# Mixed stage reordered, with the transposition of the first maxima as a fill of the PSUM ring

## The reference

```python
x = x + conv_attn(group_norm(x))          # L0: 6 heads of 16, 1024 tokens, biases rel_h and rel_w on the scores
t = tokens(x)
t = t + causal_attn(layer_norm(t))        # L1: 6 heads of 16, keys after the query masked out
t = t + moe(layer_norm(t))

def moe(x):                               # 4 experts, 96 -> 384 -> 96
    probs  = softmax(x @ gate_w + gate_b)
    masked = probs * top2_mask(probs)
    masked = masked / (sum(masked) + 1e-9)
    h = gelu(x @ w1[e] + b1[e])           # for every expert e and every token
    y = h @ w2[e] + b2[e]
    return sum_e masked[..., e] * y[e]
```

## Time and profile before

| | us |
|---|---|
| runs of the kernel before, median of 3 | 2209.66 |
| lowest and highest of them | 2201.82, 2210.24 |
| the profiled execution | 2204.84 |
| its span, first to last instruction | 2203.0 |
| TensorE busy, of that span | 1855.9 (84%) |
| VectorE busy | 1255.3 (57%) |
| ScalarE busy | 1121.6 (51%) |
| mean granted TensorE clock | 0.933 of full |

### The profile page before, as it was taken

How to read it: one execution, slowest core, us unless ns; L and a number is a source line. 1 busy time by engine, 2 the same in 40 slices (tenths; PEclk the granted TensorE clock), 3 DMA queues, 4 the chain that set the end, 5 groups by cost and what they waited for, 6 DMA issues and landing times.

```text
span 2203.0 us, 28891 instructions
## 1 busy us (share of the span) xinstructions
PE 1855.9 (84%) x9314; PEld 743.8 (34%) x9408; DVE 1255.3 (57%) x2512; ACT 1121.6 (51%) x1423; POOL 141.7 (6%) x68
## 2 busy tenths in 40 slices
PE   0279568998899988998889988999889988999848
PEld 0123223343333432343333433344323433334324
DVE  5384367736665566736675466645676456744611
ACT  0326434675456734566446734567346744555423
POOL 0000000200020000200011000200002000200020
PEclk9669769999999999999999999999899999999979
DMA  1702530263004430163002530063202530002100
GB/s 44 134 10 53 91 72 21 50 97 65 21 18 92 57 77 11 47 110 65 22 18 56 89 80 11 18 115 64 42 22 49 96 65 13 18 10 54 28 10 7
DMA packets 55741, 111.43 MB, mean 51 GB/s; under 512 B 17687, under 2 KB 18904, under 8 KB 54041
## 3 DMA queue, kind: packets, MB, share of 16 engines
q1 hardware_dynamic: 54040, 109.06, 26.3%
q10 hardware_dynamic: 1536, 0.30, 0.1%
HBM read 61.82 MB, written 34.60 MB: 44 GB/s over the span
## 4 chain that ended last, share of the span: by engine, by line
PE 67%; DVE 18%; issue 4%; ACT 4%; DMA 4%; SPq 1%; POOL 0%; DVEq 0%; POOLq 0%; ACTq 0%
PE psOM L629 15%; PE psS L574 12%; PE psT L607 8%; PE psT L606 7%; PE psT L741 6%; DVE mx L1236 6%; PE psS L755 4%; PE psT L609 3%; PE psT L536 3%; DVE mrow L1338 2%; DVE x L1347 2%; DVE qb L1365 1%; DMA qr<-negb 1%; PE psOM L561 1%; PE psT L545 1%
## 5 line engine op out<-in xcount | busy, mean ns | idle before, releaser
L968 ACT ACTIVATE probs<-psT 128x1024 f32<-128x1024 f32 (+7 forms) x768 | 622.6, 837 | 535.2 <-PE psT L607 265.9
L1236 DVE TENSOR_REDUCE mx<-psS 128x1 f32<-128x512 f32 (+3 forms) x1152 | 704.2, 643 | 305.2 <-PE psS L574 225.1
L607 PE MATMUL psT<-qb,kb 97*128 97x512 f32 x768 | 416.1, 586 | 6.9 <-DMA qb<-negr 5.9
L629 PE MATMUL psOM<-probs,v 128*32 128x512 f32 (+3 forms) x2688 | 386.2, 560 | 22.6 <-ACT probs L968 12.0
L574 PE MATMUL psS<-ka,qa 128*128 128x512 bf16 x722 | 283.4, 401 | 22.1 <-DVE mx L1236 14.0
L606 PE MATMUL psT<-qa,ka 128*128 128x512 bf16 x720 | 278.2, 386 | 11.4 <-DVE resid L1225 4.0
L741 PE MATMUL psT<-xf,w1s 97*128 97x512 f32 x384 | 193.8, 633 | 4.2 <-ACT probs L1025 2.4
L1365 DVE TENSOR_TENSOR qb<-psOM,qa 32x768 fp32r<-32x768 f32 x128 | 121.8, 952 | 127.7 <-ACT qa L1008 126.0
L609 PE MATMUL psT<-qr,kr 97*128 97x512 bf16 (+3 forms) x576 | 185.6, 349 | 5.3 <-DMA qr<-negb 1.6
L755 PE MATMUL psS<-probs,w2s 128*96 128x512 f32 x384 | 187.9, 612 | 0.0
L574 PEld LDWEIGHTS psS<-ka,qa 128*128 128x128 bf16 x768 | 71.6, 98 | 301.3 <-DVE mx L1236 265.1
(11 more groups left out here) (143 smaller groups left out, 1598.8 us busy)
## 6 DMA issues: line engine op xcount, KB each, us to landing
scr<-split SPq DMA_DIRECT2D x32, 576.0 KB, 4.3
scr<-qb SPq DMA_DIRECT2D x16, 768.0 KB, 6.7
qr<-scr SPq DMA_DIRECT2D x48, 192.0 KB, 6.8
au<-ot SPq DMA_DIRECT2D x192, 32.0 KB, 2.0
lb<-ot SPq DMA_DIRECT2D x192, 32.0 KB, 2.0
qr<-scr SPq DMA_DIRECT2D x48, 128.0 KB, 4.3
kr<-scr SPq DMA_DIRECT2D x48, 128.0 KB, 7.3
qa<-scr SPq DMA_DIRECT2D x32, 128.0 KB, 3.8
```

The costliest lines, as they stand in the source:

```text
L607: last = mm(o[:, a:b], kb[:, h, ks], qb[:, h, a:b], start=False, stop=True)
L629: last = mm(psO[j:j + 2 * HD, a - c * HALF:HALF], v[:, kt, 2 * p + hh, :], probs[:, (2 * kt + hh) % 4, a:(c + 1) * HALF], start=kt == 0, s ...
L968: A(probs[:, n % 4, q0:T], psT[:, t_slot(ts, m), q0:T], ACT.Exp).then_inc(t_free, 1)
L1236: V.reduce_max(mx[layer][:, p % 2, (h % 2) * NT + t, kc:kc + 1], psS[:, s_bank(st, fill), 0:max_cols(layer, t, kc)], AX).then_inc(s_free, 1)
```

## The change

`MIX` gets a new order, and a new step `tmax`: the transposition of the maxima of pair 0, until now the first instruction of the attention into `psM`, becomes a fill of psT in the mixed stage, and ScalarE negates the row from there and sends it. Behind it come u11, d11 and b3, so the last expert's group stands behind the last maxima. LEAD becomes 0: the eight maxima that ran in front of the scores are made within the first pair, 24 in it in place of 16. The wait for `y_free` moves from the start of the attention to the first value product, `values(0, 0)`. The other hunks are the counts of the semaphores that follow from it.

```diff
@@ -49,7 +49,7 @@
 
 
 STAGES = ("p_gn", "p_qkv0", "gn", "attn1", "p_rel", "lead", "turn", "attn0", "qkv0", "attn0b", "norm", "mix")
-LEAD = 8
+LEAD = 0
 QKV_AT = 2 * NT + 2
 
 
@@ -77,9 +77,9 @@
             for w in text.split()]
 
 
...
+MIX = seq("gate gates u0 u1 R0 d0 H0 L0 H1 L1 v0 u2 d1 v1 ln den R1 u3 d2 u4 H2 L2 u5 res H3 d3 nrm L3 u6 d4 d5 tr R2 H4 L4 q0 q1 lev V0 d6 V1 "
+          "u7 H5 L5 R3 u8 d7 H6 L6 H7 L7 u9 b0 d8 u10 b1 m0 m1 m2 m3 d9 m4 m5 m6 m7 d10 m8 m9 m10 b2 m11 m12 m13 m14 m15 tmax u11 "
+          "d11 b3")
 
 
 def there(stage, kind):
@@ -213,7 +213,7 @@
 
 def att_m(layer, p):
 
-    return ("attn1", p) if layer else ("attn0", p - 1) if p else ("lead", 0)
+    return ("attn1", p - 1) if layer else ("attn0", p - 1) if p else ("lead", 0)
 
 
 def next_layer0(it):
@@ -579,10 +579,7 @@
 
             def transpose_max(it, layer, p):
                 ms, n = att_m(layer, p)
-                if layer == 1 and p == 0:
-                    pe.wait_ge(t_free, upto("t_free", it, ms, 0))
-                else:
-                    pe.wait_ge(rowmax, upto("rowmax", it, ms, p if layer else n + 1))
+                pe.wait_ge(rowmax, upto("rowmax", it, ms, n + 1))
                 pe.wait_ge(m_free, upto("m_free", it, ms, n))
                 mm(psM[0:2 * NT, 0:P], mrow[:, p % 2, :], ident, is_transpose=True, start=True,
                    stop=True).then_inc(m_full, 1)
@@ -617,6 +614,8 @@
 
                     q0 = q_from(layer, kt)
                     if kt == 0:
+                        if layer == 1 and p == 0:
+                            pe.wait_ge(y_free, upto("y_free", it, st, 0))
                         pe.wait_ge(o_free, upto("o_free", it, st, p))
                     for hh in range(2):
                         ts, n = att_t(layer, (p * NT + kt) * 2 + hh)
@@ -633,8 +632,6 @@
                 n = PER_PAIR[layer]
                 lead = layer == 1 and next_lead(it)
                 if layer == 1:
-                    pe.wait_ge(y_free, upto("y_free", it, st, 0))
-                    transpose_max(it, 1, 0)
                     pe.wait_ge(l1_in, upto("l1_in", it, "attn1", 0))
                     for fill in range(LEAD):
                         max_scores(it, st, fill)
@@ -661,7 +658,7 @@
                     if layer == 0:
                         pe.wait_ge(negmax_in, upto("negmax_in", it, st, 16 * p))
                     else:
-                        pe.wait_ge(negmax_in, upto("negmax_in", it, st, 16 * (p + 1)))
+                        pe.wait_ge(negmax_in, upto("negmax_in", it, st, 16 * p))
                     for kt in range(NT):
                         for hh in range(2):
                             scores(p, kt, hh, between)
@@ -824,6 +821,16 @@
                         if n == 0:
                             pe.wait_ge(l1_first, upto("l1_first", it, "mix", 192))
                         first_maxima(it, "mix", n)
+                    elif what == "tmax":
+                        first_rows(it, "mix")
+
+            def first_rows(it, st):
+
+                fs = fills(st, kind_of(it))
+                reduced = len([f for f in fs[:fs.index(("max", 2 * NT - 1)) + 1] if not by_act(f)])
+                pe.wait_ge(t_free, upto("t_free", it, st, reduced))
+                o = take_mixed(it, st, ("tmax", 0))
+                mm(o[0:2 * NT, 0:P], mrow[:, 0, :], ident, is_transpose=True, start=True, stop=True).then_inc(t_full, 1)
 
             def group_means(it, st):
                 pe.wait_ge(gstat, upto("gstat", it, st, 1))
@@ -935,13 +942,24 @@
             def neg_max(it, layer, p):
                 ms, n = att_m(layer, p)
                 act.wait_ge(m_full, upto("m_full", it, ms, n + 1))
-                act.wait_ge(negmax_in, upto("negmax_in", it, ms, 16 * max(p - 1, 0) if layer else 0))
+                act.wait_ge(negmax_in, upto("negmax_in", it, ms, 16 * max(p - 2, 0) if layer else 0))
                 A(negm[layer][:, p % 2, :], psM[0:2 * NT, 0:P], ACT.Copy, scale=-1.0).then_inc(m_free, 1)
                 act.wait_ge(m_free, upto("m_free", it, ms, n + 1))
                 row = (qb_raw, qr)[layer][C:C + 1, 2 * p:2 * p + 2, :]
                 act.dma_start(row.rearrange("o h (t q) -> o (h t) q", q=P),
                               negm_raw[layer][:, p % 2, :]).then_inc(negmax_in, 16)
 
+            def first_negated(it, st):
+
+                fs = fills(st, kind_of(it))
+                fill = fs.index(("tmax", 0))
+                act.wait_ge(t_full, upto("t_full", it, st, fill + 1))
+                act.wait_ge(negmax_in, upto("negmax_in", it, st, 0))
+                A(negm[1][:, 0, :], psT[0:2 * NT, t_slot(st, fill), 0:P], ACT.Copy, scale=-1.0).then_inc(ta_free, 1)
+                act.wait_ge(ta_free, upto("ta_free", it, st, len([f for f in fs[:fill + 1] if by_act(f)])))
+                act.dma_start(qr[C:C + 1, 0:2, :].rearrange("o h (t q) -> o (h t) q", q=P),
+                              negm[1][:, 0, :]).then_inc(negmax_in, 16)
+
             def attention(it, layer):
                 st = f"attn{layer}"
 
@@ -954,7 +972,6 @@
                     A(ot[:, p, :], psO, ACT.Copy).then_inc(o_free, 1)
 
                 if layer == 1:
-                    neg_max(it, 1, 0)
                     exp_table()
                 for p in range(PAIRS):
                     next_q = layer == 0 and next_layer0(it)
@@ -1042,6 +1059,8 @@
                         keep_values(it, "mix", 0, n)
                     elif what == "rhi":
                         rel_high(it, "mix", n)
+                    elif what == "tmax":
+                        first_negated(it, "mix")
                     elif what == "up":
                         gelu(it, "mix", n)
                     elif what == "down" and n % HJ == HJ - 1:
@@ -1237,7 +1256,7 @@
                                  psS[:, s_bank(st, fill), 0:max_cols(layer, t, kc)], AX).then_inc(s_free, 1)
                     if (fill + 1) % PER_PAIR[layer] == 0:
                         dve.wait_ge(s_free, upto("s_free", it, st, fill + 1))
-                        dve.wait_ge(m_full, upto("m_full", it, st, max(p - 1, 0)))
+                        dve.wait_ge(m_full, upto("m_full", it, st, max(p - 1 - layer, 0)))
                         V.tensor_tensor(mrow[:, p % 2, :], mx[layer][:, p % 2, :, 0], mx[layer][:, p % 2, :, 1],
                                         ALU.max).then_inc(rowmax, 1)
 
```

More of the change, by code:

```diff
@@ L77, in seq @@
             for w in text.split()]
-MIX = seq("gate gates u0 u1 R0 d0 H0 L0 H1 L1 v0 u2 d1 v1 ln den R1 u3 H2 L2 d2 H3 u4 res d3 nrm L3 u5 d4 tr u6 R2 H4 L4 d5 q0 q1 V0 lev V1 "
-          "H5 L5 u7 d6 u8 R3 H6 L6 d7 H7 L7 u9 b0 d8 b1 u10 m0 m1 m2 m3 d9 m4 m5 m6 "
-          "u11 m7 m8 m9 m10 d10 m11 m12 b2 m13 m14 d11 m15 b3")
+MIX = seq("gate gates u0 u1 R0 d0 H0 L0 H1 L1 v0 u2 d1 v1 ln den R1 u3 d2 u4 H2 L2 u5 res H3 d3 nrm L3 u6 d4 d5 tr R2 H4 L4 q0 q1 lev V0 d6 V1 "
+          "u7 H5 L5 R3 u8 d7 H6 L6 H7 L7 u9 b0 d8 u10 b1 m0 m1 m2 m3 d9 m4 m5 m6 m7 d10 m8 m9 m10 b2 m11 m12 m13 m14 m15 tmax u11 "
+          "d11 b3")
 def there(stage, kind):
@@ L110, in fills @@
 def fills(stage, kind):
-    return [x for x in steps(stage, kind) if x[0] in ("up", "max", "res", "tr", "qk", "val", "val0")]
+    return [x for x in steps(stage, kind) if x[0] in ("up", "max", "tmax", "res", "tr", "qk", "val", "val0")]
 def by_act(what):
-    return what[0] in ("up", "tr", "val", "val0")
+    return what[0] in ("up", "tr", "tmax", "val", "val0")
 _ATT = {"attn0": 1, "attn1": 1}
@@ L134 @@
     "t_full": {"p_qkv0": 4, "attn1": ATT_FILLS, "attn0": QKV_AT, "qkv0": 2,
-               "attn0b": ATT_FILLS - QKV_AT, "rel": 2, "a": NE * HJ, "next_mix": 6 + 2 * NT},
+               "attn0b": ATT_FILLS - QKV_AT, "rel": 2, "a": NE * HJ, "next_mix": 7 + 2 * NT},
     "s_full": {**{s: len(m) for s, m in MAX_STEPS.items()}, "norm": 4, "a": 2 * NE},
-    "m_full": {"attn1": PAIRS, "lead": 1, "attn0": PAIRS - 1, "a": 1},
+    "m_full": {"attn1": PAIRS - 1, "lead": 1, "attn0": PAIRS - 1, "a": 1},
     "gsum_full": _GN, "gsum_free": _GN,
@@ L148 @@
     "rowmax": {"attn1": PAIRS - 1, "lead": 1, "attn0": PAIRS - 1},
-    "negmax_in": {"attn1": 16 * PAIRS, "lead": 16, "attn0": 16 * (PAIRS - 1)},
+    "negmax_in": {"attn1": 16 * (PAIRS - 1), "lead": 16, "attn0": 16 * (PAIRS - 1), "next_mix": 16},
     "p_used": {s: ATT_FILLS for s in _ATT},
@@ L159 @@
     INCS[f"{_r}_free"] = dict(INCS[f"{_r}_full"])
-INCS["ta_free"] = {"p_qkv0": 2, "rel": 2, "a": NE * HJ, "next_mix": 3}
+INCS["ta_free"] = {"p_qkv0": 2, "rel": 2, "a": NE * HJ, "next_mix": 4}
 INCS["r_free"] = {"qkv0": 2}
```

## The result

| | median us | range us | runs |
|---|---|---|---|
| before | 2207.97 | 2201.82 to 2210.24 | 4 |
| changed | 2266.91 | 2260.78 to 2268.59 | 4 |

The changed kernel is slower: 1.027 times the time of before, 95% interval 1.0247 to 1.0293, 59 us. The forecast was 2260, range 2215 to 2292. The profiled execution has a span of 2266.1 us, 63.1 more than that of before.

The account below looks back on a forecast made before the run. TensorE, busy 84%, was taken to bound the kernel through waits in its program order. Four back edges at +8.6 us, three other boundaries (16.4 together) and ends of 3.6 summed to +54.4, giving 2260 us, range 2215 to 2292.

Parts of the forecast that it names:

- The reading of the back edge: At four taken loop branches, TensorE's 4880 ns idle is the branch; removing the y_free wait there is worth nothing.
- C: From last expert's transposition (b3) to next image's first scores: -4.6 us at back edges, -6.9 at the three others.
- The rival that the wait behind the branch holds it up: At back edges, the branch shrinks to 83 ns once the wait is gone; faster, 2192 us, 7%.
- A: From fourth up product (u3) to first expert's transposition (b0): +1.0 us, with TensorE newly idle 3.9 us before bias product R3.
- I take the boundary at 1056 us as the pattern: One boundary between two images, a back edge, was the base: 43.25 us from u3 to b0, 22.99 from b0 to b3.
- B: From first (b0) to last expert's transposition (b3): +8.2 us; +6.5 from work in series at full clock, rest half clock.
- D: First pair of the attention, taking over eight maxima: +4.0 us at back edges, +3.5 at the three others.
- Ends: First image, without experts, +1 us; last image, losing cover of u11's Gelu and waiting at d6, +2.6; together 3.6.
- The clock did not hold: Rival that TensorE's clock stays at full throughout the boundaries: 2217 us, 10%.
- It spread in part: Rival that half clock spreads from R3's wait to b0 and from m11 into the first pair: 2290 us, 18%.

## Why the prediction was right

**The reading of the back edge** held: the branch stood where it was said, and two kernels show it from both sides, the one with the wait for y_free back and the one with TensorE's loop written out. Its size did not: 3703 ns where 4880 was carried over, so C was -5.6 on average at edges and not -4.6. The rival that the wait behind the branch holds it up is out twice: the branch stays long without the wait, and with the wait put back it is no longer (3.5 to 4.0 us). At the three others C was -6.8, as forecast (-6.9).

**A, +1.0, was the worst term**: +3.6 on average in the six turns with bias products, -2.5 in turn 6. The mechanism was right to the tenth: R3 waits 3.90 us, 3.9 forecast, and comes 5.8 us after u7, 5.7 forecast. What failed is "I take the boundary at 1056 us as the pattern". That turn is one of three in which A is 43.2 with the clock at half for 6.8 us; in the three others before has 39.9 at full clock, in the same kernel with the same waits. With the mean of the six, 41.6, the same walk gives +2.7 of the measured +3.6, and 0.5 of the rest is turn 0 alone, where the clock fell twice (47.70 us at 0.86). The half clock that followed the 3.9 us (u8 3.78 at 0.50, d7 3.30 at 0.57: 3.3 us lost) was only the upper end of the walk, "up to 2.8 later"; it costs nearly as much as the wait. The experiments add that without both the head is a gain.

**B, +8.2, measured +8.8 on average.** The last reduction ended 23.9 us after b0, 23.3 forecast; from there to b3 7.8 us, 6.1 and the half clock's 1.7 forecast. The middle taken between 0 and 3.4 for the clock came out almost exactly, and not because both products were slowed by half as much: in the boundary shown u11 took the whole loss (3.56 at 0.53), d11 none (1.96 at 1.00). Over the seven boundaries the agreement is luck, since two errors cancel. At four boundaries the transposition came 22.3 to 22.4 us after b0, so the last reduction was some 1 us earlier than forecast; at the three others half clock had also fallen early in the stretch (d9 3.1 to 3.3 us at 0.57 to 0.62), and it came 24.0 to 24.2 us after b0. From the transposition to b3 it was 7.6 to 7.7 us at three boundaries and 9.2 to 9.5 at four, where d11 too ran at half clock (3.5 to 3.7 us at 0.50 to 0.56). With 22.3 and the forecast's 6.1 us for that tail, B without any half clock would be an estimated 28.4, not 29.4, and the clock cost 3.3 of the 31.7 on average, not 1.7.

**D, +4.0 at edges, measured +3.25**; at the others 3.5 against 2.9. The parts were wrong and cancelled, which is luck. At the last two boundaries the clock was at full through the pair (1.00), and D was still 21.77 and 21.75 us. The prediction's own terms give 18.79 + 0.7 = 19.5 there, and it called full clock in the pair a sign that D falls. So the moved maxima cost some 2.3 us more than forecast: TensorE waits 1.8 us for VectorE's reductions in that pair, where 0.8 was allowed. At the edge shown (0.89) half clock cost the 1.2 us between 21.77 and 22.99, not the 3.3 of the sum. The kernel with eight leading maxima again shows what the prediction's sum implied but didn't say, that C and D at an edge are one exchange worth nothing.

**Ends.** The last image cost 1.8, 2.6 forecast: u11's Gelu shows (1.17 us ahead of d11), but d6 behind d5 waited only 0.77. In the first image the transposition stands 3.0 us later than before, 1.9 of it already ahead of any changed step. The scores come 2.5 us after it, not 4.3, and the first pair takes 23.2 us in place of 19.5, so the second pair starts 4.9 us later, where +1 was forecast.

**The rivals.** The branch did not shrink to 83 ns; at the exit it had been 83 before, and that row was the argument. The clock did not hold: 0.84 over B and 0.89 over D in the boundary shown. It spread in part: d11 was at half clock at four of seven boundaries, B reached the rival's size once (+10.6 at 3 to 4, clock 0.76), and the first pair had no half clock at the last two (1.00). The total was right partly because errors cancelled. Over the boundaries A was forecast 13 us and B 4 us too low, C 4 us and D 5 us too high, and the whole came out 8 us above the sum.

## What to carry to other kernels

A wait that ends under a longer one is worth nothing, and the profile names only the longer. In the changed kernel the wait for y_free put back changed C at the four back edges by at most 0.3 us and at the three others by 2.5 to 2.8; in the kernel before, the profile named "issue" with 4.63 us, and with TensorE's loop written out the additions with 2.58. So look at the passages where the longer one is missing (here the loop's exit) before taking a wait's idle time as the gain. The chain of short dependent products at the end of this stage cost its waits (1.39, 1.11 and 0.85 us in the boundary shown) and half clock in the products between them: B was 31.66 us at a granted clock of 0.84, and 25.00 at 1.00 with the end of the stage in the old order. In this kernel such a chain belongs between other work and not behind the last reduction. When an order of many moved steps loses, take it apart before dropping it: one misplaced group (H5, L5 and R3) carried 7 us for each image, and the rest of the head was worth 24 us in all.
